# A selective scan by token halves with its input product on GpSimd, and level 0's key rows placed pair by pair from ScalarE's queue

## The reference, cut to what matters

```python
# level 0, first layer (the second: the same with a causal mask, then a mixture of experts)
scores = jnp.einsum('bhqd,bhkd->bhqk', q, k) / np.sqrt(HEAD_DIM)
attn = jax.nn.softmax(scores, axis=-1)
out = jnp.einsum('bhqk,bhkd->bhqd', attn, v)

# level 1: 256 channels, 16 states
delta = jax.nn.softplus(dt_raw @ W_dt + b_dt)
A = -jnp.exp(A_log)
dA = jnp.exp(delta[..., None] * A)
dBx = delta[..., None] * Bp[:, :, None, :] * xv[..., None]
# h[t] = dA[t] * h[t-1] + dBx[t], for every channel and state
y = jnp.einsum('bldn,bln->bld', h, Cp)
y = y + xv * D
return y @ W_out
```

## Time and profile before

| | |
|---|---|
| median of 3 runs | 4062.47 us (4061.41 to 4076.33) |
| the profiled execution | 4063.1 us, span in the trace 4061.4 us |
| busy over the span | PE 81%, DVE 76%, ACT 63%, POOL 11% |
| mean granted TensorE clock | 0.897 of full speed |
| level 0, first attention: end of setup, loop | about 59 to 88 us and from 88 us on |
| level 0, causal attention: the same | about 796 to 826 us and from 826 us on |
| scan block | about 1629 to 1918 us |
| projection block behind it | 1918 to 1928 us |

### The profile page before, as it was taken

The page is one execution under the profiler, slowest core; times in us unless marked ns, Lnnn a source line. Parts: engine busy times, 40 slices in busy tenths (PEclk is TensorE's granted clock), DMA queues, the critical chain, the costliest instruction groups (busy, mean ns, idle before and its releaser), DMA issues. The chain is left out here.

```text
span 4061.4 us, 129963 instructions
## 1 busy us (share of the span) xinstructions
PE 3294.3 (81%) x55226; PEld 2143.1 (53%) x55226; DVE 3074.8 (76%) x3739; ACT 2550.6 (63%) x4883; POOL 429.8 (11%) x1465
## 2 busy tenths in 40 slices
PE   2999999479997996555665639999999999999728
PEld 1566666235555673222444416666666666666415
DVE  4999999358893114998454449999999999999753
ACT  1799999337776344221211119999999999999622
POOL 0000000011000000000003001111111111111120
PEclk7899999779998997778876859999999999999858
DMA  5000000310000001330007874555455555554410
GB/s 113 9 7 9 7 9 5 88 25 11 9 7 2 24 18 47 145 116 29 6 5 117 242 195 120 124 123 125 121 128 128 120 130 120 129 127 117 108 33 11
DMA packets 208869, 305.77 MB, mean 75 GB/s; under 512 B 96508, under 2 KB 140994, under 8 KB 203150
## 3 DMA queue, kind: packets, MB, share of 16 engines
q1 hardware_dynamic: 203614, 292.37, 28.9%
q0 software_dynamic: 4688, 5.24, 0.6%
HBM read 228.17 MB, written 60.40 MB: 71 GB/s over the span
## 5 line engine op out<-in xcount | busy, mean ns | idle before, releaser
L843 ACT ACTIVATE channels_qk<-psum 128x512 f32<-128x512 f32 (+1 forms) x3906 | 2100.6, 594 | 286.2 <-PE psum L688 200.4
L905 DVE TENSOR_REDUCE l2f_chunk_max<-psum 128x2 f32<-128x1024 f32 x1176 | 1359.5, 1217 | 52.2 <-PE psum L663 48.4
L905 DVE TENSOR_REDUCE chunk_max<-psum 128x2 f32<-128x1024 f32 (+2 forms) x832 | 918.5, 1157 | 85.9 <-PE psum L663 46.1
L663 PE MATMUL psum<-l2f_k_parts,l2f_q_parts 48*128 48x512 bf16 x2352 | 715.0, 387 | 38.2 <-DVE l2f_chunk_max L905 26.8
L709 PE MATMUL psum<-channels_qk,l2f_v_and_ones 128*9 128x128 f32 x18432 | 718.2, 274 | 14.1 <-issue 14.1
L688 PE MATMUL psum<-l2f_q_parts,l2f_k_parts 51*128 51x128 bf16 x9224 | 727.6, 217 | 2.0 <-ACT l2f_minus_max_rows L885 0.9
L663 PE MATMUL psum<-k_parts,q_parts 48*128 48x512 bf16 (+3 forms) x1664 | 425.1, 382 | 130.3 <-DMA q_parts<-q_rows_dram 93.2
L688 PEld LDWEIGHTS psum<-l2f_q_parts,l2f_k_parts 51*128 51x128 bf16 x9224 | 496.3, 94 | 41.9 <-ACT channels_qk L843 39.2
L709 PE MATMUL psum<-channels_qk,v_and_ones 128*9 128x128 f32 x12544 | 491.8, 275 | 1.8 <-ACT channels_qk L843 0.5
L709 PEld LDWEIGHTS psum<-channels_qk,l2f_v_and_ones 128*9 128x9 f32 x18432 | 396.7, 90 | 122.6 <-issue 16.5
L688 PE MATMUL psum<-q_parts,k_parts 51*128 51x128 bf16 x6272 | 430.6, 218 | 29.2 <-DMA q_parts<-minus_max_rows 10.6
(11 more groups left out here) (479 smaller groups left out, 3004.4 us busy)
## 6 DMA issues: line engine op xcount, KB each, us to landing
l2f_k_parts<-l2f_k_parts_dram SPq DMA_DIRECT2D x604, 192.0 KB, 3.6
l2f_v_and_ones<-expert_v_dram SPq DMA_DIRECT2D x148, 288.0 KB, 4.3
l1a_bc_rows<-ssm_rows_dram SPq DMA_DIRECT2D x16, 1024.0 KB, 5.5
expert_v_dram<-l2f_v_and_ones SPq DMA_DIRECT2D x8, 1152.0 KB, 4.4
channels_qk<-ssm_rows_dram SPq DMA_DIRECT2D x8, 1024.0 KB
expert_q_dram<-heads_out SPq DMA_DIRECT2D x8, 1024.0 KB
l2f_q_parts<-l2f_gathered_q_parts SPq DMA_DIRECT2D x456, 16.0 KB
k_parts<-k_rows_dram SPq DMA_DIRECT2D x4, 1536.0 KB
```

The lines of the kernel that those rows point to most:

```text
L663: last = nc.tensor.matmul(c.ps[:, 2 * (n % 2) + j, 0:width], at.q[64 * j:64 * j + ROWS, tile % SLOTS, pair, :], kx(tile)[64 * j:64 * j + R ...
L843: nc.scalar.activation(at.prob[:, s % 4, j, 0:kts, :].rearrange("p k q -> p (k q)"), c.ps[:, ring.bank(i, n), 0:kts * 2 * P], ACT.Exp, sca ...
L905: v.tensor_reduce(at.mx[:, 4 * g + 2 * pp:4 * g + 2 * pp + 2, chunk], c.ps[:, 2 * (n % 2):2 * (n % 2) + 2, 0:span.width(tile, chunk)], X, ...
```

## The change

Two parts that touch different stages.

**Level 0's keys.** `place_keys` issues 16 DMAs of 192 KB, one per pair and partition range, in the order of the pairs, from ACT's queue, behind ACT's last instruction of the layer's block and a wait for the key stores. Each group of two pairs has a semaphore. The block's end waits no more for the keys; in the loop PE waits for group g's keys in front of the first unit of tile 0's first pass of that group.

**The scan.** It goes over the first 1024 tokens for all states and both channel halves (32 steps), then over the second 1024 (32 more). The decay is written to PSUM (two banks per step, two sets in turn, banks 4 to 7), so the output takes four banks (0 to 3) and is copied out by ACT between the token halves. The product with B moves to GpSimd. The last state column of a step is kept in `carry` by a one-column copy on ACT and starts the scan of the second token half. `a` is used in place, so `load_a` goes. Input and state have 4 buffers of 1024 columns; the rows have 8 buffers of half rows (512 KB a DMA), the first two loaded ahead. The loops are unrolled. The block behind copies only the second half (4 copies), and PE starts on the first half without a wait.

```diff
 def place_keys(at, eng, keys_placed):
-    for j in range(2):
-        eng.dma_start(at.kx[64 * j:64 * j + ROWS, 0, :, :], at.k_rows_dram[j].rearrange("p d r t -> (d r) p t")).then_inc(keys_placed, 16)
+    for pair in range(NPAIR):
+        for j in range(2):
+            eng.dma_start(at.kx[64 * j:64 * j + ROWS, 0, pair, :], at.k_rows_dram[j, pair].rearrange("d r t -> (d r) t")).then_inc(keys_placed[pair // 2], 16)
...
                     if routed:
                         pe.wait_ge(k_loaded[tile % 2][g], (tile // 2 + 1) * KL)
+                    elif tile == 0:
+                        pe.wait_ge(keys_placed[g], 16 * 2 * 2)
...
-            sp.wait_ge(k_stored, 16 * 2 * 3)
-            place_keys(at, sp, keys_placed)
             sp.wait_ge(q_stored, 16 * 2 * 3)
-            sp.wait_ge(keys_placed, 16 * 2)
...
+            act.wait_ge(k_stored, 16 * 2 * 3)
+            place_keys(at, act, keys_placed)
+    return keys_placed
...
+            @block.scalar
+            def _(act):
+                for step in range(2 * S):
+                    h, n = step % 2, step % S // 2
+                    if step >= 2:
+                        act.wait_ge(scanned, step - 1)
+                    nc.scalar.activation(decay(step), delta[:, h, tokens(step)], ACT.Exp, scale=a[:, h, n:n + 1]).then_inc(da_ready, 1)
+                    if 2 <= step < S + 2:
+                        nc.scalar.activation(carry[:, step - 2:step - 1], u[:, (step - 2) % U, TH - 1:TH], ACT.Copy).then_inc(carried, 1)
+                    if step == S + 2:
+                        act.wait_ge(added, S)
+                        for g in range(2):
+                            nc.scalar.activation(dx[:, g, 0:TH], ps[:, 2 * g:2 * g + 2, :].rearrange("p b n -> p (b n)"), ACT.Copy).then_inc(y_copied, 1)
+
+            @block.gpsimd
+            def _(pool):
+                for step in range(2 * S):
+                    b_row, _ = rows.wait(pool, step // 2)
+                    if step >= 2:
+                        pool.wait_ge(hc_ready, step - 1)
+                    if step >= U:
+                        pool.wait_ge(carried, min(step - U + 1, S))
+                    nc.gpsimd.tensor_tensor(u[:, step % U, :], dx[:, step % 2, tokens(step)], b_row, ALU.mult).then_inc(u_ready, 1)
...
+                for step in range(2 * S):
+                    _, c_row = rows.wait(dve, step // 2)
+                    if step == S:
+                        dve.wait_ge(carried, S)
+                    dve.wait_ge(da_ready, step + 1)
+                    dve.wait_ge(u_ready, step + 1)
+                    v.tensor_tensor_scan(u[:, step % U, :], decay(step), u[:, step % U, :],
+                                         0.0 if step < S else carry[:, step - S:step - S + 1], ALU.mult, ALU.add).then_inc(scanned, 1)
+                    dve.wait_ge(scanned, step + 1)
+                    if step >= U:
+                        dve.wait_ge(added, step - U + 1)
+                    v.tensor_tensor(hc[:, step % U, :], u[:, step % U, :], c_row, ALU.mult).then_inc(hc_ready, 1)
...
+                for step in range(2 * S):
+                    if step == S:
+                        pe.wait_ge(y_copied, 2)
+                    if step % S == 0:
+                        for h in range(2):
+                            for b in range(2):
+                                nc.tensor.matmul(ps[:, 2 * h + b, :], diag[:, h, :], xv[:, h, step // S * TH + b * 512:step // S * TH + (b + 1) * 512],
+                                                 start=True, stop=False)
+                    pe.wait_ge(hc_ready, step + 1)
+                    for b in range(2):
+                        last = nc.tensor.matmul(ps[:, 2 * (step % 2) + b, :], c.ident[:, :], hc[:, step % U, b * 512:(b + 1) * 512],
+                                                start=False, stop=step % S >= S - 2)
+                    last.then_inc(added, 1)
```

More of the change, by code:

```diff
@@ L1443, in _ @@
                     sp.wait_ge(ssm_stored, 16)
-                    for k in range(2):
-                        rows.load(sp, k, k)
+                    for m in range(2):
+                        rows.load(sp, m)
                 @block.tensor
@@ L1524, in _ @@
             def _(act):
-                for k in range(NC):
+                for k in range(2, NC):
                     for h in range(2):
-                        nc.scalar.activation(y[:, h, k * 512:(k + 1) * 512], ps[:, 4 * h + k, :], ACT.Copy).then_inc(y_ready, 1)
+                        nc.scalar.activation(y[:, h, k * 512:(k + 1) * 512], ps[:, 2 * h + k - 2, :], ACT.Copy).then_inc(y_ready, 1)
             @block.tensor
@@ L1586, in _ @@
             def _(sp):
[L1587 to L1599 removed]
+                for m in range(2, AHEAD):
+                    rows.load(sp, m)
@@ L1601, in _ @@
+                for m in range(AHEAD, S):
+                    sp.wait_ge(hc_ready, 2 * (m - AHEAD) + 2)
+                    rows.load(sp, m)
             @block.scalar
             def _(act):
-                def decays(r, k):
-                    act.wait_ge(rows.loaded[k], r * L + L)
-                    for h in range(2):
-                        act.wait_ge(scanned, r * (2 * K) + (2 * k + h + 1))
-                        nc.scalar.activation(da[:, h, :], delta[:, h, :], ACT.Exp, scale=anow[:, k, h:h + 1]).then_inc(da_ready, 1)
```

114 lines of the change are left out of this document (34 added, 80 removed).

## The result

The changed kernel takes **3997.98 us** (median of 4 runs, 3988.02 to 3999.63), the kernel before beside it 4061.94 (4 runs): ratio 0.9827, 95% interval 0.9811 to 0.9842, a gain of 64 us or 1.7%. The forecast was 3972, a gain of 91; the range held the time. The profiled execution took 3996.37 us, its span is 3994.6 (before 4063.1 and 4061.4).

A forecast was written before the change was run, and what follows sets the result against it. DVE was taken to bound the scan and DMA engines the two key setups. Gains of 53.6 (scan), 6.7 (tail) and 31.0 (keys) sum to 91.3, taking 4063.1 to 3972 us, range 3950 to 4002.

The forecast's parts named there:

- The scan's step: Scan, per state and channel half of 1024 columns: 3.51 us, 64 steps, 224.6 us; 53.6 us gained.
- The two paths: Scan step: DVE's 2.28 + 1.23 and GpSimd's hand-over 0.08, product 2.33, then 1.09 of product with C; both about 3.51 us.
- The rival of the held scan: Scan: every scan held by GpSimd's product of the next step, 5.92 us a step, 4126 us in all; chance 0.07.
- The start of the scan: Start of the scan's block: first scan at about 1631.7, after GpSimd's first product, ACT's table load and first decay.
- its rule, that one input in SBUF is safe: Scan: a DVE instruction with at most one SBUF input does not contend with a GpSimd instruction that reads SBUF.
- The tail: From the scan's last product to the projection's last addition: 10.9 us instead of 17.6, 6.7 us gained.
- The keys: Both attention setups: first scores at 72.5 and 811, 15.5 us gained at each, together 31.0, bounds 7 to 36.
- the bound "behind all keys": First attention's first scores if they come behind all keys: 75.5 us with fast keys, 85.5 with slow ones.
- the lowest bound: Earliest first scores of the first attention, query rows with nothing in their way: given as 69.7 us.
- the forecast's own range: Whole kernel: 3953 us (scan at 3.33 a step, keys at their best) to 3990; forecast given 0.60.
- the rival in which PE becomes the bound: Scan: PE at its lower clock throughout, four instructions take 4.3 us, 275 us for 64 steps, 4022 in all; chance 0.03.

The follow-up runs named there:

- E3: Changed kernel with the scan's decay in an SBUF buffer instead of PSUM, waits as they are; 4131.11 us (kernel before on that chip 4079.03).
- E5: Changed kernel with GpSimd waiting for both diagonal products of DVE before its first product with B; 3980.06 us.
- E9: The changed kernel run again unaltered, on one chip with later runs; 4004.93 us, ratio 0.9817 to the kernel before.
- E6: Changed kernel with key pairs 0 to 3 from ScalarE, then first query rows, pairs 4 to 7 and second query rows from SyncE; 3978.52 us.
- E8: Changed kernel with the keys in the old two transfers of 1.5 MB, from ScalarE's queue, both awaited before the first scores; 4006.37 us.
- E1: Kernel before with only the new key loads and waits, old scan; 4057.32 us, ratio 0.9954 to the kernel before.
- E4: Changed kernel with the product with B back on DVE, halves and PSUM decay kept; 4104.52 us (kernel before on that chip 4079.03).
- E12: As E11, but GpSimd's product with B waits only for its buffer, so it may run ahead of the scan; 3998.04 us, one run.
- E2: Kernel before with only the new scan, keys in the two large transfers as before; 4028.95 us, ratio 0.9879 to the kernel before.
- E7: Changed kernel with the same key loads by pairs and waits, issued from SyncE's queue ahead of the query rows; 3990.61 us.
- E11: Changed kernel, GpSimd waiting for the diagonal products, all keys from SyncE's queue, only pairs 0 and 1 ahead of first query rows; 3991.07 us, ratio 0.9794.

## Why the prediction was right in kind and 26 us too far

Against the profiled execution the forecast was 91.3 us of gain, and 66.7 came. The difference by its own steps:

- **The scan's step**, 3.51 forecast, 3.56 measured: 64 steps, 3.3 us. The two paths did meet, as the text said; that of GpSimd is the longer. Its terms 0.08 + 2.33 + 1.09 measured 0.12 + 2.35 + 1.08 (the hand-over was the one too small); the scan's 2.28 was right, and so was taking the PSUM operand as free and not held, which E3 shows by taking it away. The rival of the held scan had the right price in kind (5.92 a step; E3's other order gives 5.42), but not its condition.
- **The start of the scan**: the forecast had the first scan 2.6 us behind the block's first instruction (1631.7 against 1629.1), measured were 4.64 (1615.04 against 1610.40). These 2.0 us are a hold that the prediction missed (E5 gives 1.6 of the 4.64 back): it left the two diagonal products out of its sum, and by its rule, that one input in SBUF is safe, they would have been. They have one and were held. The Trainium skill, "SBUF — State Buffer", section "Who interferes with whom", names `tensor_scalar` among the operations that can take the shared ports by themselves, and says that whoever issues first has them for the whole instruction. The 4.71 us here, the 0.48 of E5 and E3's order agree with both sentences. The rule for one input, in the same section of the Trainium skill, excepts the modes in which an instruction takes both ports, and the prediction told it without that exception.
- **The tail**: 6.7 forecast, 7.0 measured.
- **The keys**: 31.0 forecast, 23.4 measured. This is the step that failed: "I take 72.5, near the first" of the bounds. Its only reason was the speed of the keys' form; that the query rows would land ahead of the last keys had no row for it. They came at 76.3, near the bound "behind all keys" with the keys fast (75.5). That the figures meet so well is partly luck: the keys ran at 185 GB/s over this stretch and not 225, but were issued 2.0 us sooner. In E9 they ran at 215 and 231, near the forecast, and the scores still came 17.7 and 17.2 us behind the first issue, where 72.5 asks for 13.8. So the speed was a fair guess and the order of landing was wrong. E6 shows that moving the rows ahead of half the keys brings 5.8 and 6.7 us. By its own terms the lowest bound is 66.6 + 2.8 = 69.4, not 69.7, and 72.5 lies midway between 69.7 and 75.5. The Trainium skill, "DMA: Bandwidth & Descriptors", section "Queues, rings and completion order", has the queues of an engine take turns by packets. The trace shows little of such turns: 43 packets of the rows' queue in the 7 us in which 1.34 MB of keys moved. Why so few of them move is open.
- **Given back ahead of the scan**: the lead was 23.4 us at the causal scores and 18.7 at the scan's block. Windows of the changed kernel, then of the kernel before:

```profile
823.00:843.00 20.00, 15.40 (x130) 6.21 (x129) 7.63 (x13) 5.79 (x14) 3.19 (x16) 0.50 0.05 11
843.00:863.00 20.00, 17.06 (x240) 8.13 (x239) 13.22 (x20) 9.79 (x25) 3.98 (x20) 0.84 0.05 12
```
```profile
846.00:866.00 20.00, 15.39 (x130) 6.18 (x128) 7.62 (x13) 5.78 (x14) 3.18 (x16) 0.50 0.05 12
866.00:886.00 20.00, 16.95 (x268) 8.48 (x266) 15.38 (x22) 11.54 (x29) 3.98 (x20) 1.00 0.05 12
```

  The windows lie 23 us apart, as the work does. In the first of each the two kernels do the same at the lower level (0.50). In the second the kernel before has the full clock from the start (1.00, 268 matmuls), the changed one for part of it (0.84, 240). This need not come from the change: from the first causal maximum to the scan's block, whose engines run the same code in all, the kernel before took 801.9 us, the changed one 806.7, the changed one again in E9 801.2, and all traces 796 to 808.
- **Behind the projection**: the lead was 74.0 us there and 66.8 at the end, in code that is the same. On one chip this part took 2138 to 2141 us (E5 to E8), on another 2149 to 2159 (E1 to E4), on a third 2152 to 2158 (E9 to E12); before and changed, 2134 and 2141. The 7 us are of the size of that spread. A cause in the change is neither shown nor excluded.

The sum is 3.3 + 2.0 - 0.3 + 7.6 + 4.7 + 7.2 = 24.5 of the 24.6 us. So 12.6 us are the forecast's own, and the other 12 arose in stretches whose code the change does not touch.

Two figures beside the sum were also off. The low end of the forecast's own range, 3953, is 3955 by its terms (64 x 0.18 and 5.3 below 3971.8). And the rival in which PE becomes the bound doubled a row of 8.56 us for 16 instructions that had already run partly at the lower clock (granted 0.83 from 1890.6 to 1899.2). Behind it, from 1909.05 on and at a granted clock of 0.50, PE's weight loads follow each other 0.85 us apart, so four instructions take 3.4 us by this estimate and PE would have stayed below the step of 3.51.

## What to carry to other kernels

Moving DVE's work to GpSimd pays, by these runs, only if the DVE instruction that runs beside it is not kept apart from it: here a PSUM operand for the scan was worth 119 us, and either half of the design without the other (E3, E4) was slower than no change. Look also at the small single-input instructions at the block's start, and let GpSimd wait until they are through: 1.6 us in E5. When a small load decides when an engine starts, issue it ahead of the large ones: a queue of its own did not carry it past 3 MB. And compare two rates only after the same code has been read at both places and in a second execution: here it varied from 193 to 231 GB/s by itself (changed and E9).

## What was not expected of the hardware

- Two `tensor_scalar` of 128 columns, each with one tensor input, which is in SBUF, took 4.71 us instead of 0.48 beside running GpSimd products (E5 undoes it).
- A scan with both inputs in SBUF that starts first makes GpSimd's 2.35 us product 4.21 (E3).
- 3 MB of keys move at 128 to 132 GB/s in two transfers and at 180 to 251 in sixteen, with the DMA engines full each time (before, E2, E8 against changed, E1, E3, E4, E5, E7, E9). The queue that issues them makes no difference that shows; what spreads the rate of the sixteen is open.
- Query rows in pieces of 256 B, on a queue of their own, land behind 3 MB of keys that another queue issued before them: the first scores come 11.7 us behind the rows' issue, and 7.6 and 5.1 us with half and a quarter of the keys ahead (changed, E6, E11).
- Dependent DVE instructions of 1024 columns have pauses of 0.04 to 0.13 us between them (E4), 0.26 in a step of three.
